# The first stage's opening rewritten: skip term added to the kernel rows, rows first in the queue, variances by group, first two turns in two banks

## What is computed

```python
x = x + jnp.tanh(g_xattn[0]) * _L0_xattn_ref(ctx_2048, ctx_2048, _layernorm(x, axis=-1), L0_xattn_ssm_kernel, L0_xattn_D, 8)

def _L0_xattn_ref(k, v, q, ssm_kernel, D, head_dim):
    kv = jnp.einsum('bhil,bhjl->bijhl', k_, v_)          # k and v are both the context
    kv_f = jnp.fft.rfft(kv, n=fft_size)
    kernel_f = jnp.fft.rfft(ssm_kernel, n=fft_size)
    y = jnp.fft.irfft(kv_f * kernel_f, n=fft_size)[..., :L]
    out = y + kv * D[None, None, None, :, None]          # D is the skip term
    out = jnp.einsum('bijhl,bhil->bjhl', out, q_)
```

## Time and profile before

| | us |
|---|---|
| median of three runs | 908.05 |
| lowest, highest | 906.32, 909.58 |
| the profiled execution's own time | 910.07 |
| its span from first to last instruction | 908.3 |
| mean granted TensorE clock in it | 0.988 of full |

### The profile page before, as it was taken

One profiled execution on the slowest core, in us unless ns is written; L12 is line 12 of the kernel. 1 busy time (PEld: TensorE's weight loads), 2 busy tenths in 40 slices (PEclk: granted clock), 3 DMA queues, 4 the chain that ended last, 5 costly groups with the idle time before them and its releaser, 6 DMA issues.

```text
span 908.3 us, 13885 instructions
## 1 busy us (share of the span) xinstructions
PE 877.6 (97%) x4747; PEld 717.3 (79%) x4768; DVE 600.4 (66%) x1238; ACT 532.5 (59%) x916; POOL 133.2 (15%) x108
## 2 busy tenths in 40 slices
PE   6799999999999999989999989999999999999997
PEld 5799887777788888867777767878788888888886
DVE  5689764465654665579999865657755566666564
ACT  3225243344554344357777757777677867777774
POOL 5799300001012020012121310000000000000000
PEclk9799999999999999989999999999999999999999
DMA  8204150524532442013343234444444344444433
GB/s 293 86 1 135 36 157 18 158 73 160 168 123 82 144 143 59 24 30 114 111 125 102 82 116 125 139 136 140 140 140 143 95 140 139 139 149 151 147 122 105
DMA packets 70117, 106.47 MB, mean 117 GB/s; under 512 B 9216, under 2 KB 34176, under 8 KB 69664
## 3 DMA queue, kind: packets, MB, share of 16 engines
q1 hardware_dynamic: 69328, 105.44, 37.1%
q10 hardware_dynamic: 720, 0.14, 0.1%
HBM read 96.84 MB, written 8.72 MB: 116 GB/s over the span
## 4 chain that ended last, share of the span: by engine, by line
PE 87%; DVE 5%; POOL 2%; DMA 2%; ACT 1%; issue 1%; SPq 1%; DVEq 0%; ACTq 0%; POOLq 0%
PE bank L682 38%; PE bank L718 29%; PE bank L1525 3%; PE bank L1536 2%; PE bank L1516 2%; PE bank L1169 1%; PE bank L1168 1%; PE bank L1428 1%; PE bank L366 1%; PE bank L1166 1%; PE bank L1182 1%; DMA toeplitz<-in_kpad 1%; PE bank L1545 1%; PE bank L1510 1%; PE bank L347 1%
## 5 line engine op out<-in xcount | busy, mean ns | idle before, releaser
L479 ACT ACTIVATE y_hi<-y 128x512 fp32r<-128x512 f32 x200 | 124.0, 621 | 82.0 <-DVE y L562 81.4
L576 DVE TENSOR_TENSOR y<-y,gate_rows 128x512 f32<-128x512 f32 x124 | 85.8, 692 | 120.4 <-ACT y L468 117.6
L718 PE MATMUL bank<-y_hi,w_hi 128*128 128x512 f32 x400 | 157.3, 393 | 2.0 <-DVE y_lo L312 1.5
L718 PE MATMUL bank<-y_lo,w_hi 128*128 128x512 f32 x400 | 156.6, 391 | 0.0
L718 PE MATMUL bank<-y_hi,w_lo 128*128 128x512 f32 x400 | 155.9, 390 | 0.0
L312 DVE TENSOR_TENSOR y_lo<-y,y_hi 128x512 fp32r<-128x512 f32 x196 | 134.3, 686 | 30.0 <-ACT y_hi L479 29.6
L462 ACT ACTIVATE activated<-bank 128x512 f32<-128x512 f32 x136 | 81.1, 597 | 80.8 <-PE bank L682 76.2
L682 PE MATMUL bank<-x_hi_first,w_hi 128*128 128x512 f32 x264 | 106.2, 402 | 0.7 <-DVE w_lo L307 0.7
L682 PE MATMUL bank<-x_hi_first,w_lo 128*128 128x512 f32 x264 | 104.2, 395 | 0.0
L682 PE MATMUL bank<-x_lo_first,w_hi 128*128 128x512 f32 x264 | 104.1, 394 | 0.0
L682 PE MATMUL bank<-x_hi_last,w_hi 128*128 128x512 f32 x264 | 104.0, 394 | 0.0
(11 more groups left out here) (155 smaller groups left out, 1372.3 us busy)
## 6 DMA issues: line engine op xcount, KB each, us to landing
gate_rows<-gates SPq DMA_DIRECT2D x156, 256.0 KB, 3.7
w_raw<-in_wu SPq DMA_DIRECT2D x68, 256.0 KB, 2.6
w_raw<-in_wu SPq DMA_DIRECT2D x32, 384.0 KB, 4.2
k_blocks<-k_parts SPq DMA_DIRECT2D x128, 64.0 KB, 2.4
k_parts<-xn_split SPq DMA_DIRECT2D x32, 128.0 KB
v_slot<-in_v_rows SPq DMA_DIRECT2D x16, 256.0 KB, 2.7
ctx_windows<-in_ctx_win SPq DMA_DIRECT2D x3, 1024.0 KB, 10.8
toeplitz<-in_kpad SPq DMA_DIRECT2D x4, 512.0 KB, 9.4
```

Source lines behind the costliest of these rows:

```text
L479: act.activation(mem.yhi[:, K % S, :], mem.y[:, K % S, :], ACT.Copy).then_inc(s_yh, 1)
L576: dve.tensor_tensor(mem.y[:, K % S, :], mem.y[:, K % S, :], gate, ALU.mult).then_inc(s_yd, 1)
L718: last = pe.matmul(acc(s)[:, c, :], w_[:, Nu % S, wc], y_[:, K % S, :], start=(n == 0 and m == 0), stop=(n == U - 1 and m == 2), skip_grou ...
```

## The change

The skip term is no longer added to the loaded tables. The 16 padded kernel rows (24 KB) are loaded into SBUF, DVE adds D to one column (one instruction), ACT stores the rows into a new DRAM tensor `k_mid`, and SP waits for that store before it issues the four table loads from there. The 16 DVE instructions and their two constants go.

The order of the DMAs is new: kernel rows, the first group's x and two window quads ahead of the wait; then tables and the other two quads; then the gates' values (which stood on ACT's queue before); then x and windows of group 1 and of the others. The host lays x out so that a group is read as 4 KB for each partition where it was four pieces of 1 KB.

Variances, deviations and shifts are made group by group: group 1 after weigh(2), group 2 after weigh(5), group 3 after weigh(10). Two of the four blocks of group 0 are normalised on DVE. The two turns of group 0 follow the first convolution instead of the third, and go into two banks, so the second doesn't wait for the first to be copied out. 10 + 4 dummy matmuls (`keep_clock`) replace 16. The addition of halves for n = 3 is dropped, and reduce(1) takes all eight pieces of that half instead (12 passes instead of 8).

```diff
         def part_of(phase, part):
-            first = BPB if phase == "a" else 2 * BPB
+            if phase == "a":
+                return slice(BPB * part, BPB * part + BPB)
+            first = 2 * BPB
...
+            WHOLE = 3
+            MOMENTS_AT = {2: 1, 5: 2, 10: 3}
...
+            def query_bank(g, half):
+                return bk(6) if g == 0 and half == 1 else x_bank
...
                 def kernel_table(hq):
-                    src = bass.AP(kpad.tensor, kpad.offset + 4 * hq * 384, [[1, P], [384, 4], [1, D]])
+                    src = bass.AP(k_mid.tensor, k_mid.offset + 4 * hq * 384, [[1, P], [384, 4], [1, D]])
...
+                sp.dma_start(kern[:], kpad).then_inc(s_ca, 16)
+                rows(0)
                 window_quad(0)
-                kernel_table(0)
-                rows(0)
-                for hq in range(1, 4):
-                    window_quad(hq)
+                window_quad(1)
+                sp.wait_ge(s_ks, 16)
+                for hq in range(4):
                     kernel_table(hq)
-                for i in range(1, NG):
+                    if hq + 2 < 4:
+                        window_quad(hq + 2)
+                sp.dma_start(graw[:, 0:2], g_x.partition_broadcast(P)).then_inc(s_tl, 16)
+                sp.dma_start(graw[:, 2:4], g_f.partition_broadcast(P)).then_inc(s_tl, 16)
+                rows(1)
+                window_group(1)
+                for i in range(2, NG):
                     rows(i)
-                for g in range(1, NG):
+                for g in range(2, NG):
                     window_group(g)
...
                 pairs(0)
-                pairs(1)
                 pool.wait_ge(s_mh, 1)
                 deviations(pool, "a", 0)
                 shifts(pool, "a", 0)
+                pairs(1)
                 pairs(2)
                 pairs(3)
                 for q in range(1, NQ + 1):
...
-                    if q + 3 < NQ:
+                    if 4 <= q and q + 3 < NQ:
                         pairs(q + 3)
-                    if q == 2:
-                        deviations(pool, "a", 1)
-                        shifts(pool, "a", 1)
+                    if q == 6:
+                        deviations(pool, "a", 3)
+                        shifts(pool, "a", 3)
                     for n in (2 * q - 2, 2 * q - 1):
                         if n % 4 != 3:
                             halves(n)
+                    if q in (1, 3):
+                        deviations(pool, "a", q // 2 + 1)
+                        shifts(pool, "a", q // 2 + 1)
+                    if q < 4:
+                        pairs(q + 3)
...
                 act.dma_start(ident[:], ident_c).then_inc(s_c, 16)
-                act.dma_start(anti[:], anti_c).then_inc(s_ca, 16)
-                act.dma_start(dbc[:], d_skip.partition_broadcast(P)).then_inc(s_ca, 16)
-                act.dma_start(graw[:, 0:2], g_x.partition_broadcast(P)).then_inc(s_tl, 16)
-                act.dma_start(graw[:, 2:4], g_f.partition_broadcast(P)).then_inc(s_tl, 16)
+                act.dma_start(dcol[:], d_skip.rearrange("(h a) -> h a", a=1)).then_inc(s_ca, 16)
+                act.wait_ge(s_td, 1)
+                act.dma_start(k_mid, kern[:]).then_inc(s_ks, 16)
...
-                keep_clock(pe, bk(6), 16)
+                keep_clock(pe, bk(6), 10)
                 for g in range(NG):
                     for r in range(8):
                         convolve(g, r // 2, r % 2)
-                        if g == 0 and r == 2:
+                        if g == 0 and r == 0:
+                            keep_clock(pe, bk(6), 4)
                             for half in range(2):
                                 turn(0, half)
...
-                def table(hq):
-                    dve.wait_ge(s_kt[hq], 16)
-                    for h in range(4 * hq, 4 * hq + 4):
-                        last = dve.scalar_tensor_tensor(TM[:, h, 0:P], anti[:], dbc[:, h:h + 1], TM[:, h, 0:P], ALU.mult, ALU.add)
-                    last.then_inc(s_td, 1)
+                def skip_added():
+                    dve.wait_ge(s_ca, 32)
+                    dve.tensor_tensor(kern[:, P - 1:P], kern[:, P - 1:P], dcol[:], ALU.add).then_inc(s_td, 1)
+
+                def first_rows_normed():
+                    dve.wait_ge(s_r, 1)
+                    for b in range(2):
+                        last = dve.tensor_scalar(xn[:, 0, b, :], Xa[:, b, :], mv[:, b, 0:1], rstd[:, b:b + 1], ALU.subtract, ALU.mult)
+                    last.then_inc(s_nd, 1)
```

More of the change, by code:

```diff
@@ L62, in build @@
 def build(nc, x, ctx_win, k_rows, v_rows, g_x, g_f, kpad, d_skip, wu0, rw0, eb0, wu1, rw1, br1,
-          ident_c, anti_c, identb_c, causal_c, out):
+          ident_c, identb_c, causal_c, out):
     top = ExitStack()
@@ L1079, in q_windows @@
                         act.wait_ge(s_z, 8 * (g - 1))
-                    src = x_bank.rearrange("p (n i) -> p n i", i=HD0)
+                    src = query_bank(g, half).rearrange("p (n i) -> p n i", i=HD0)
                     for copy in range(2):
@@ L1097, in normed @@
                 def normed(g):
-                    if g < 2:
-                        act.wait_ge(s_sh, g + 1)
-                    else:
+                    act.wait_ge(s_sh, g + 1)
+                    if g >= 2:
                         act.wait_ge(s_xt, 2 * (g - 1))
-                    for j in range(BPB):
+                    for j in range(2 if g == 0 else 0, BPB):
                         b = BPB * g + j
@@ L1108, in a_scalar @@
                 squares(0)
-                act.wait_ge(s_tl, 32)
-                act.activation(tg[:], graw[:], ACT.Tanh).then_inc(s_tg, 1)
                 squares(1)
@@ L1116, in a_scalar @@
                 squares(3)
+                act.wait_ge(s_tl, 32)
+                act.activation(tg[:], graw[:], ACT.Tanh).then_inc(s_tg, 1)
                 for q in range(NQ - KR):
@@ L1141, in turn @@
                     pe.wait_ge(s_n, g + 1)
-                    if 2 * g + half > 0:
+                    if g == 0:
+                        pe.wait_ge(s_nd, 1)
+                    else:
                         pe.wait_ge(s_qx, 2 * g + half)
                     for j in range(BPB):
-                        last = pe.transpose(x_bank[:, j * P:(j + 1) * P], xn[:, g % 2, j, half * P:(half + 1) * P], ident[:])
+                        last = pe.transpose(query_bank(g, half)[:, j * P:(j + 1) * P], xn[:, g % 2, j, half * P:(half + 1) * P], ident[:])
                     last.then_inc(s_xt, 1)
@@ L1154, in convolve @@
                         if g == 0:
-                            pe.wait_ge(s_td, hq + 1)
+                            pe.wait_ge(s_kt[hq], 16)
                     if n >= 3:
@@ L1180, in reduce @@
                     for half in range(2):
-                        for k in range(4):
+                        pieces = 8 if 2 * q + half == WHOLE else 4
+                        for k in range(pieces):
                             last = pe.matmul(acc_bank(q)[:, half * P:(half + 1) * P], Z[:, q % ZR, half, k, :], ident[:],
-                                             start=(k == 0), stop=(k == 3), is_transpose=True, skip_group_check=True)
+                                             start=(k == 0), stop=(k == pieces - 1), is_transpose=True, skip_group_check=True)
                     last.then_inc(s_ac, 1)
                 pe.wait_ge(s_c, 16)
-                keep_clock(pe, bk(6), 16)
+                keep_clock(pe, bk(6), 10)
                 for g in range(NG):
@@ L1257, in residual @@
                     dve.bn_stats(stats[:, b, :], Xa[:, b, :]).then_inc(s_sd, 1)
-                dve.wait_ge(s_ca, 32)
-                table(0)
-                input_moments(0)
-                dve.wait_ge(s_st, st.n)
-                variances(dve, "a", 0)
-                negated(dve, "a", 0)
-                for hq in range(1, 4):
-                    table(hq)
-                dve.wait_ge(s_tg, 1)
+                skip_added()
+                group_moments(0)
+                first_rows_normed()
                 for g in range(NG):
```

43 lines of the change are left out of this document (26 added, 17 removed).

## The result

| | before | changed |
|---|---|---|
| median (lowest, highest) us | 908.91 (906.32 to 909.86), 6 runs | 902.71 (899.79 to 904.81), 6 runs |
| ratio of times, 95% interval | | 0.9935 [0.9919, 0.9951] |
| the profiled execution's own time | 910.07 | 904.81 |
| its span | 908.3 | 902.9 |
| mean granted TensorE clock | 0.988 | 0.992 |

By the ratio the change wins 5.9 us (0.65%), where 9.0 were forecast. The time lies in the forecast's range, near its end.

What follows compares the result with a forecast made beforehand. TensorE's idleness in the opening was the time to win, POOL and TensorE nearly equal limits after it. pairs(7) 9.2 us earlier less 0.2 gave 9.0, carried to the end: 908.05 to 899 us, forecast 896.5 to 901.5, wider range 895.5 to 903.5.

Steps and rivals of the forecast that it cites:

- When the first table lands: Opening: column DMA, DVE addition, store and table load in series put the first table at 10.5 us (9.5 to 13.2).
- From there to n = 3: Opening after the first table: nothing waits, convolution n = 3 starts at 17.3 instead of 22.13, plus 1.0 for slow clock.
- Group 1's queries: Group 1's variances, deviations and shifts end at 24.3 us; its turn comes at 26.5 instead of 37.62.
- POOL takes over: POOL's queue of 12.6 us behind group 1's shifts starts pairs(7) at 36.9, 9.2 earlier; reduce(3) stalls 2 to 3.
- the clock term: Opening: TensorE at its slow pace after idling could cost up to 3.2 us; 1.0 was put in.
- From pairs(7) to reduce(10): POOL's work gains 1.44 us for group 3's deviations, 1.3 of short waits go: net 0.1 to 0.2 later.
- The sum: −9.2 + 0.2 = −9.0 us at reduce(10), carried to the end: median 908.05 becomes 899.
- The rule that I weighed: Shared port lock: GpSimd blocks two-input DVE instructions; at worst three times 1.05 us added for deviations, sum −6; not counted.
- A dearer round trip: Rival: the store through DRAM waits in the rings, first table 2 to 4 us later, 902 us; chance 0.13.
- the table's late landing: Slower rival: first table lands at 23.2 us, past break-even at 19.5, giving 912 us; chance 0.02.
- That POOL and DVE block each other: Rival: blocking at small instructions of groups 1 and 2 delays pairs(7) by up to 4 us: 903; chance 0.10.

Runs made afterwards that it cites:

- the second measurement: The changed kernel without an edit, timed again beside the kernel before: 905.07 us, ratio 0.9959.
- the last kernel: The changed kernel with 18 opening dummies, no DVE addition for n = 23, router split one half step earlier: 899.39 us, 0.9897 of before.

## Why the prediction was right, and where it was wrong

**When the first table lands.** Forecast 10.5, measured 10.39. That it fits so well is partly luck, as the two halves erred against each other: the store took 1.5 where I had 2.1, the table 4.1 where I had 3.6.

**From there to n = 3.** Forecast 17.3 and up to 1.0 of clock, measured 18.77, with the half pace that I put down as unsure: 2.26 against 1.22 from the first pass to the one behind the eight, and 1.75 for eight dummies. "Nothing waits" was right.

**Group 1's queries.** Shifts done at 23.75 (forecast 24.3), first turn at 25.91 (26.5).

**POOL takes over.** pairs(7) at 36.06 (36.9), 10.0 earlier in place of 9.2; the stall of reduce(3) 2.53 (2 to 3). The run with shared variances shows the hole as the cause, and the run with more dummies gives the clock term as 0.8 to 1.1.

**From pairs(7) to reduce(10).** Forecast 0.2 later, measured 0.6. reduce(10) at 76.33 (76.7).

**The sum.** The step that failed is "Behind it all waits are between engines, and nothing is tied to the start of the program ... So the 9.0 carries to the end." Of the 9.4 us at reduce(10) 4.0 were gone two steps later. An equal shift of every engine would have carried. But DVE and GpSimd weren't shifted equally: at the addition of n = 23 DVE had been 0.15 us ahead of GpSimd's short instruction and was now 1.13 behind it, because `neg_mean` had been held for 2.08 us at 65.46. That this was the loss is shown by the trace with more dummies, which has the same addition, an unheld `neg_mean` and no loss, and by the two traces with a held `neg_mean` in which the split was moved (2.7 us back) or the addition dropped as well (3.3). The two runs without the addition whose `neg_mean` wasn't held don't show it.

**Luck in the number.** The forecast of 9.0 us was of the gain at reduce(10), and there it was right for its reasons. The measured time lies in the range only because the range reached to 903.5; the 4.0 us that were lost had no place in the sum, and the second measurement, 905.07, lies outside.

**The rule that I weighed.** The prediction set the row of 13.73 against it and priced the rule at 3 us, for the deviations. The runs show DVE held up by GpSimd at other places: DVE's two-input instructions took 1.91 in place of 0.74, 1.02 in place of 0.22, and 0.77 in place of 0.30 each for twelve. In the kernel before, five of the first six additions of halves on DVE took 1.6 to 2.1 us. The Trainium skill (SBUF — State Buffer, Who interferes with whom) states just this for a DVE instruction with two SBUF inputs against a GpSimd one that reads SBUF, and that issue order decides who blocks. The traces agree on both: GpSimd's took 0.94 for 0.49 where DVE had begun first. `neg_mean`, which has one input, was held too, 2.08 in place of 0.16. The row of 13.73 is still unhindered, and in the changed kernel the addition at 68.83 took 0.69 beside a root of 1.64 that had begun at 68.71; why GpSimd's reciprocal root doesn't hold DVE, no run here tells. My fault was to read the rule for the instructions that the change adds, and not for those whose meeting it shifts; the row of 4.04 in the trace of before would have told that pairs, unlike the root, do block.

**The rivals.** A dearer round trip and the table's late landing fell: it landed at 10.39. That POOL and DVE block each other was listed, at 903, but for the small instructions of groups 1 and 2 and ahead of pairs(7). Those of group 1 ran free (0.17 and 0.16) and those of group 2 were held (0.85 and 1.31 at 29.07 and 29.83), but pairs(7) was not late by it. The size came true at another place: the small instruction that mattered was the next stage's `neg_mean` at 65.46.

**What the parts are worth.** The prediction took the 16 additions as some 8 us of DVE and the variances as the hole behind. The runs show that they pay together and little one by one: at reduce(10) the kernel rows alone win 1.6 us, everything but them 2.6, everything but the variances by group 4.3, and all of it 9.4. With x first, the additions fall beside three pairs; without x first and variances by group, group 1's turn still waits.

**Open.** The second measurement of the changed kernel was 0.24% above the first, and their intervals overlap little. The granted clock from 380 to 400 us, in a later stage, averaged 0.91 in the changed kernel's first trace, 0.83 in its second, 1.00 in the one without the addition and 1.00 with the last kernel; whether such stretches at half clock are the whole difference between measurements wasn't shown. From reduce(12) to the end the fourteen traces take 809.0 to 813.2 us. The second trace of the changed kernel was 3.8 us ahead of that of the kernel before at reduce(12) and lost all of it behind (spans 905.2 and 905.1), so a single pair of traces doesn't tell this gain. How often `neg_mean` is held, and how much of the spread of times comes from it, isn't known. The new order of loads, the normalising on DVE and the addition dropped for n = 3 were not tried by themselves.

## What to carry to other kernels

When a change shifts one engine's work against another's, go through the pairs of instructions that lie near each other behind the change and can block each other, here a DVE addition out of SBUF and a long GpSimd instruction, and ask which begins first now. Follow a late engine back to where it fell behind: here that was a tiny instruction 11 us ahead of the loss, and hundredths of a microsecond decided it. A gain at a stage's middle is a gain at the end only if the order of such meetings stays. A short wait of TensorE can cost twice, when the clock falls behind it. And before an edit is credited with a trace that looks better, see whether the trace had left the old course ahead of the edited place.

## What the runs showed of the hardware

- An addition of 128x512 out of SBUF took 0.69 us by itself (at 91.16 in the changed kernel) and 1.91 when it began 0.68 us behind a GpSimd instruction of 2.04. Where it began first it took 0.74, and GpSimd's 0.94 in place of 0.49.
- A `neg_mean` of 128x8 took 2.08 to 2.10 us in six traces and 0.16 in seven. Where it started within 0.03 us of a GpSimd instruction of 2.03 to 2.06, it came out either way.
- A store of 24 KB from SBUF to DRAM released the next load 1.54 us after its issue. The load of 512 KB in overlapping windows from it took 4.1 us into a queue nearly empty, against 6.3 to 10.3 behind other loads.
- TensorE's granted clock was mostly at 1.2 GHz from 10.39 to 14.24 (0.57 and 0.54 in the mean) after 20 short passes and 3.0 us of idleness, and at 2.4 after 36 and 2.0 us. In the changed kernel it fell again behind the wait of 2.30 us (0.51 from 82.54 to 85.82), as behind those of 2.29 in its second trace and in the run with the tables on DVE (0.51 and 0.50). It did not fall behind the wait of 2.30 in the run with one bank (1.00), nor behind the one of 1.12 in the run with the router early.
- With the tables on DVE, 20 passes and only 1.33 us of idleness, the eight passes of the first convolution took 2.53 us to the next instruction, the slow pace, though the granted clock of that stretch reads 1.00. With the kernel rows alone, 32 passes and 2.3 us of idleness, they took 1.30.
